# Transposing the routed rows by DMA, from SBUF to SBUF, in place of TensorE and ScalarE

## The reference

```python
def _L0_ffn_ref(x, A, B, W, bias):
    vecs = jnp.einsum('arh,bsh->bsar', A, x)          # 64 experts, rank 16
    arrows = jnp.linalg.norm(vecs, axis=-1)
    _, idx = jax.lax.top_k(arrows, TOPK)              # TOPK = 4
    routes = jax.nn.one_hot(idx, arrows.shape[-1], dtype=x.dtype).sum(-2) / TOPK
    v = jnp.einsum('bsa,bsar->bsr', routes, vecs)
    delta = jnp.einsum('bsa,ajr,bsr->bsj', routes, B, v)
    base = jnp.einsum('bsh,jh->bsj', x, W) + bias
    return base + delta
...
def step(h, inp):
    dA_t, Bu_t, C_t = inp
    h = dA_t * h + Bu_t
    y = jnp.sum(h * C_t[:, None, :], axis=-1)
    return (h, y)
...
x = x + 0.5 * _L0_ffn_ref(_layernorm(x, axis=-1), L0_ffn_A, L0_ffn_B, L0_ffn_W, L0_ffn_bias)
x = x + _L0_attn_ref(_layernorm(x, axis=-1), L0_attn_W_xproj, L0_attn_W_dt, L0_attn_b_dt, L0_attn_A_log, L0_attn_D_param)
x = x + 0.5 * _L0_ffn_ref(_layernorm(x, axis=-1), L0_ffn_A, L0_ffn_B, L0_ffn_W, L0_ffn_bias)
```

## Time and profile before

| | |
|---|---|
| median of 3 runs | 3119.35 us (3117.05 to 3121.25) |
| the profiled execution's own time | 3113.97 us |
| its span, from first to last instruction | 3112.0 us |
| PE busy | 2721.8 us (87%) |
| POOL busy | 2326.4 us (75%) |
| DVE busy | 2299.5 us (74%) |
| ACT busy | 1548.5 us (50%) |
| mean granted clock of PE | 0.972 of full speed |
| moved by DMA | 340.03 MB, mean 109 GB/s |

### The profile page before, as it was taken

The page is one execution under the profiler, slowest core; times in us unless marked ns, Lnnn a source line. Parts: engine busy times, 40 slices in busy tenths (PEclk is TensorE's granted clock), DMA queues, the critical chain, the costliest instruction groups (busy, mean ns, idle before and its releaser), DMA issues. The chain is left out here.

```text
span 3112.0 us, 41383 instructions
## 1 busy us (share of the span) xinstructions
PE 2721.8 (87%) x14528; PEld 1271.8 (41%) x14592; DVE 2299.5 (74%) x2912; ACT 1548.5 (50%) x2906; POOL 2326.4 (75%) x694
## 2 busy tenths in 40 slices
PE   0599899899989989999989899888999988988999
PEld 0255444344444434444433344434444433433444
DVE  5533688688888878878768887878878888788633
ACT  1333466555546645555454555545555554454321
POOL 0000699788989998989879898889988999889300
PEclk9999999999999999999989999999999999999999
DMA  4012333343335243433343343333343344333110
GB/s 185 14 43 77 123 102 119 113 139 123 100 123 156 81 128 102 139 122 110 115 131 126 103 123 116 111 122 107 121 136 124 116 125 129 122 102 118 48 41 34
DMA packets 173586, 340.03 MB, mean 109 GB/s; under 512 B 12353, under 2 KB 88257, under 8 KB 173378
## 3 DMA queue, kind: packets, MB, share of 16 engines
q1 hardware_dynamic: 156482, 303.82, 30.4%
q10 hardware_dynamic: 16896, 33.56, 3.6%
HBM read 234.04 MB, written 103.28 MB: 108 GB/s over the span
## 5 line engine op out<-in xcount | busy, mean ns | idle before, releaser
L414 POOL TENSOR_TENSOR mreg<-mreg 128x2048 f32<-128x2048 f32 x256 | 1160.0, 4532 | 41.3 <-DVE hst L966 41.2
L406 POOL TENSOR_TENSOR mreg<-mreg 128x1024 f32<-128x1024 f32 x340 | 794.5, 2359 | 417.4 <-DMA mreg<-delta_scratch 339.2
L724 ACT ACTIVATE pA<-mreg,nA 128x512 f32<-128x512 f32 x1024 | 696.5, 687 | 688.6 <-DVE mreg L963 615.2
L963 DVE TENSOR_TENSOR_SCAN mreg<-pA,hst,mreg 128x512 f32<-128x512 f32 x768 | 944.1, 1267 | 116.7 <-ACT pA L724 86.9
L437 PE MATMUL po<-wB,uT 128*128 128x512 f16 x2048 | 493.1, 391 | 51.7 <-ACT uT L662 51.7
L437 PE MATMUL po<-wW,xT 128*128 128x512 f16 x2048 | 469.8, 380 | 8.0 <-issue 7.0
L437 PE MATMUL pv<-wA,xT 128*128 128x512 f16 x2048 | 468.5, 382 | 1.2 <-ACT xT L645 1.2
L401 POOL TENSOR_TENSOR mreg<-mreg 128x2048 f32<-128x2048 f32 x86 | 389.7, 4532 | 52.7 <-issue 52.6
L963 DVE TENSOR_TENSOR_SCAN mreg<-pA,cst,mreg 128x512 f32<-128x512 f32 x256 | 315.0, 1267 | 38.9 <-ACT pA L724 34.9
L523 PE MATMUL py<-mreg,Em 128*32 128x512 f32 x2048 | 279.4, 618 | 59.0 <-DVE mreg L975 32.5
L437 PEld LDWEIGHTS po<-wB,uT 128*128 128x128 f16 x2048 | 201.0, 100 | 296.6 <-ACT uT L662 59.4
(11 more groups left out here) (108 smaller groups left out, 2637.4 us busy)
## 6 DMA issues: line engine op xcount, KB each, us to landing
mreg<-delta_scratch SPq DMA_DIRECT2D x256, 512.0 KB, 5.4
delta_scratch<-mreg ACTq DMA_DIRECT2D x128, 256.0 KB
xin<-x SPq DMA_DIRECT2D x32, 512.0 KB, 4.7
x_scratch<-xin SPq DMA_DIRECT2D x32, 512.0 KB, 7.2
xnT_scratch<-auxs SPq DMA_DIRECT2D x32, 512.0 KB, 2.8
mreg<-xnT_scratch SPq DMA_DIRECT2D x64, 256.0 KB, 4.3
mreg<-bc_scratch SPq DMA_DIRECT2D x64, 256.0 KB, 5.7
yT_scratch<-mreg SPq DMA_DIRECT2D x64, 256.0 KB, 6.6
```

Of the source, the lines that this page charges most:

```text
L406: pool.tensor_tensor(Hr[:, G % NH, 2 * h:2 * h + 2, :], u, b.broadcast_to([P, 2, CT]), ALU.mult).then_inc(s_bm, 1)
L414: pool.tensor_tensor(h, h, Cr[:, g, :].unsqueeze(1).broadcast_to([P, 4, CT]), ALU.mult).then_inc(s_cm, 1)
L724: nc.scalar.activation(pA[:, i % 2, :], Dr[:, 2 * (n % NPR) + i % 2, :], ACT.Exp, scale=nA[:, c:c + 1]).then_inc(s_dA, 1)
L963: V.tensor_tensor_scan(h, pA[:, i % 2, :], h, before, ALU.mult, ALU.add).then_inc(s_sc, 1)
```

## The change

PE's `routed_blocks` and ACT's copy go. In their place `routed_copy` issues one DMA transpose for each part from ACT's queue, which reads `un2` in SBUF and writes `uT` in SBUF; each part's landing raises a semaphore of its own, `s_uc[0]` or `s_uc[1]`, by 16. Both calls of `routed_copy` now stand together in ACT's `unit`, behind `decays(5, 7)` and ahead of `softplus(a, 0)`; before, they stood on both sides of `decays(10, 11)` and `delta_out`. `norm_blocks` no longer waits for the copies, and `squares` waits for both landings.

```diff
             def norm_blocks(b, half):
                 if half == 0:
                     pe.wait_ge(s_xn, b.u + 1)
-                pe.wait_ge(s_uc, max(b.u * 2 - half, 0))
...
-            def routed_blocks(a, part):
-                pe.wait_ge(s_u, a.u * 2 + 1 + part)
-                for k in range(KD):
-                    last = nc.tensor.transpose(pth[part][:, k * P:(k + 1) * P], un2[:, part, k, :], idh[:, :])
-                last.then_inc(s_uT, 1)
-
             def routed(a, nb, third):
                 if nb == 0 and third != 1:
-                    pe.wait_ge(s_uc, a.u * 2 + (1 if third == 0 else 2))
+                    pe.wait_ge(s_uc[third // 2], 16 * a.u + 16)
...
                     pe.wait_ge(s_ya, y.v * 2 + 2)
-                routed_blocks(a, 0)
                 states(a, 2)
                 if late:
                     pe.wait_ge(s_pc, late.w + 1)
-                routed_blocks(a, 1)
                 routed(a, 0, 0)
...
                 if nb == 0:
-                    act.wait_ge(s_uT, b.u * 2)
+                    act.wait_ge(s_uc[0], 16 * b.u)
+                    act.wait_ge(s_uc[1], 16 * b.u)
...
             def routed_copy(a, part, y_done):
-                act.wait_ge(s_uT, a.u * 2 + 1 + part)
+                act.wait_ge(s_u, a.u * 2 + 1 + part)
                 if part == 0:
                     act.wait_ge(s_yT, 2 * y_done)
-                nc.scalar.activation(uT[:, part, :, :].rearrange("p k t -> p (k t)"), pth[part], ACT.Copy).then_inc(s_uc, 1)
+                act.dma_start_transpose(uT[:, part, :, :], un2[:, part, :, :].rearrange("p k q -> p (k q)")).then_inc(s_uc[part], 16)
...
                 decays(5, 7)
+                routed_copy(a, 0, a.f2s + (b is not None and b.kind == 2))
+                routed_copy(a, 1, 0)
                 softplus(a, 0)
...
                 delta_copy(a, 0)
-                routed_copy(a, 0, a.f2s + (b is not None and b.kind == 2))
                 decays(10, 11)
                 delta_out(a, 0)
-                routed_copy(a, 1, 0)
```

More of the change, by code:

```diff
@@ L203, in build @@
         s_vec = sem("s_vec"); s_sq = sem("s_sq"); s_n2 = sem("s_n2"); s_mk = sem("s_mk"); s_gm = sem("s_gm")
-        s_u = sem("s_u"); s_uT = sem("s_uT"); s_uc = sem("s_uc")
+        s_u = sem("s_u"); s_uc = [sem(f"s_uc{n}") for n in range(2)]
         s_out = sem("s_out"); s_res = sem("s_res")
```

## The result

The changed kernel takes 3269.25 us (3260.33 to 3272.76) against 3120.3 us: the ratio is 1.047, with a 95% interval of 1.045 to 1.050. It is slower by 4.7%, where 3076 us was forecast. The time lies outside the range too.

The account below looks back on a forecast made before the run. PE and POOL, about equally busy, were taken to bound the scan stage. Gains of 40 us there and 7 before, less 4 behind, off 3113.97 gave 3071; the median's 5.4 more made 3076 us, range 3030 to 3225.

Parts of the forecast that it names:

- The length of the landing: Time from when ACT can issue part 0 to its landing: put at 4.5 us, with ends 2.5 and 6.6.
- my own table: Scan-stage gain by landing time: 100 us at 2.5, 66 at 4.5, 30 at 5.5, a loss of 14 at 6.6.
- Units 58 to 62: Behind the scan, `uT` is read until `y_blocks` ends: 1.2 us slower a unit, a loss of 4 us.
- Units 1 to 4: Before the scan, 10 us between issue and need: 1.6 us gained each, 0.8 in unit 0, together 7.
- What passes through: Scan stage: 0.6 of PE's 66 us shortens the kernel, 40 us, as waits for other engines grow.
- the gain: PE's saving over 53 scan units: mean 1.90 us usable, 100.5 together; 66 us with a 4.5 us landing.
- My rival of this kind: POOL and the loop behind it set the scan stage's length; only 3 us gained, 3116 us; chance 0.16.
- ACT's queue: Two issues of 0.54 us replace two copies of 1.02 in ACT's unit: 1 us less work, no cost.
- the threshold of 1.7 us an issue: Bound below which ACT's issues cost nothing, from `projection_copies` ending before the products start in unit 33.
- ACT's queue is held: A transpose holds ACT 2.5 us an issue, delaying `projection_copies` and DVE's scans; 83 us lost, about 3204; chance 0.07.
- Late landing: Transposes share DMA engines with SP's broadcasts and land after 8 us; 103 us lost, 3222 us; chance 0.13.
- Traffic: 34 MB on top of 340 slows the step sizes' round trip: costed at nothing, at most 9 us.

## Why the prediction was wrong

**The length of the landing: sized too long.** I took 4.5 us from the nearest rows, and the median is 3.3 us (the mean in the scan units 4.1). By my own table that made the change look worse than it was on this point, so this is not the step that failed. Units 58 to 62, where I expected 1.2 us more each, kept their length. Units 1 to 4 gained 1.1 us of the 1.6 and unit 0 1.7 in place of 0.8. Of the two figures of the Trainium skill that I set side by side, the 1309 ns for a 128x128 block ("VectorE: DVE Perf Modes", "The three transpose paths") does not add up over blocks: eight of them land in 3.1 us. The advice to use TensorE where PSUM will do as the destination, which I had put into the same section, stands in that page's "Rules for kernel authors"; this case agrees with it, by 4.7% with the DMAs on ACT's queue and by 0.35% with them on SP's.

**What passes through: the first step that failed.** "I let 0.6 of the gain through." It was none in the scan stage (2595.8 us against 2579.9 with the work gone altogether). Already the gain was sized too large: without the transposes the products start 1.5 us earlier on average, where I had counted on 1.9. My rival of this kind put the cause on POOL. Work added on POOL costs 0.3 to 0.4 of its length; the branch that PE meets next is ACT's and DVE's, from the seventh decay to `xn`. It ended 0.05 us ahead of PE in unit 33. I compared PE's wait for `uT` with what would let it start earlier, and did not read on to PE's next wait, L429 in the middle of `routed`, which had no idle time because both branches ended together there, as they did within 0.3 us in 20 of the 53 units.

**ACT's queue: the step that turned the sign.** "ACT costs nothing as long as an issue is under 1.7 us." Three terms of it were off. The issue holds 1.25 us and more and not 0.54, which was the price of a plain DMA. "The two copies that go give it back before the end of the unit" is wrong: without the copies and without any DMA, `xn` ends 27.7 us after `choose`, as with them, so their going gives nothing back on that branch. And the threshold of 1.7 us an issue was worked out from `projection_copies` alone. In 34 of the 53 scan units both issues were under it, and a hold of 2.2 us a unit, where it allowed 3.4, cost 100 us with no DMA at all. The rival "ACT's queue is held" named the right queue, with a chance of 0.07, but kept the threshold: it priced two issues of 2.5 us at 1.6 us a unit (53 x 1.6 is 85, which gives its 3204, and not 83), and by its arithmetic the 3.05 us measured on average would have cost nothing. The runs gave 0.86 to 0.94 us for each us of hold at 1.1, 2.2 and 2.75 us a unit. With 0.9, 3.05 us x 53 x 0.9 = 145 us stand against the 148 by which the stage is longer than without the transposition, and the 164 by which it is longer than in the kernel before.

**Late landing.** Not the cause in the changed kernel: 11 us of waits. It became one with the issues at the old places, where 344 us of waits were for landings.

**Traffic.** Costed at nothing, at most 9 us. The stage was 5 us longer with the DMAs from SP than with no transposition, which is within the spread, so nothing speaks against it.

## What to carry to other kernels

An engine with half of its time idle can be the one that sets the pace, if its work at one point of the loop lies between two hand-overs; before an instruction is put on its queue, find the next consumer that comes right on time (idle time nought, started within a tenth of a us of its operand) and follow that branch back. To learn what the removal of work can bring at most, run the kernel without it, and to learn what a place in a queue costs, put a known hold there: the two runs answer here what no reading of the sums did. The hold costs by what stands behind it in that kernel, so it is to be put into the kernel with the change as well as into the one before. A DMA's price is two numbers, its hold of the issuing queue and its landing, and the hold of one kind of DMA is no measure for another.

## What was not expected of the hardware

- An issue of a DMA transpose from SBUF to SBUF holds its queue 1.21 to 1.25 us for 1 to 8 blocks of 128x128 float16 on ACT early in the kernel; 16 blocks, beside a load of 4096 KB, held it 2.06 us. On SP, for 8 blocks, it is 1.23 us at the least, too, and 1.30 in the median. A plain store of 256 KB holds ACT's queue 0.53 us in the median.
- The hold was longer where large transfers had been issued shortly before. In the changed kernel, all 17 issues of part 1 in the 53 scan units that took over 1.6 us (up to 5.6) had one or two of SP's broadcasts of 512 KB in the 7 us before them, against 8 of the 36 shorter ones. With the issues at the old places, all 36 issues of part 1 right behind two stores of 256 KB on ACT's own queue took 2.2 to 6.4 us, and the 17 others 1.25 to 1.54. That the transfers are the cause is inferred from this coincidence; no run varied it alone.
- The view of the DMA queues counts 135,168 packets more on ACT's queue for 128 transposes, 1056 each, against 132 for a store of 256 KB (16,896 for 128).
